# For the last pair of images, TensorE takes seven of the convolution's nine taps and VectorE two

## What is computed

```python
def block(x):
    # 1. depthwise 3x3 convolution whose nine taps depend on the image
    l = ln_over_channels(x)
    wt = softmax(max(l) @ w2.T + b2 - (mean(l) @ w1.T + b1), axis of length 1)   # 9 per image and channel
    x = x + (conv3x3(l, wt) + bias + l)
    # 2. mixture of 8 experts, 2 per token; a token is one pixel with its 128 channels
    t = tokens(x); n = ln_over_channels(t)
    top_w, top_i = top_k(n @ Wg + bg, 2); top_w = softmax(top_w)
    t = t + (sum(top_w[e] * (gelu(n @ W1[e] + b1[e]) @ W2[e] + b2[e]) for e in top_i))
    return images(t)
```

## Time and profile before

| | before |
|---|---|
| median of 3 runs | 1597.68 us (1597.11 to 1598.95) |
| span of the profiled execution | 1597.2 us |
| PE (TensorE) busy | 1476.3 us, 92% |
| DVE (VectorE) busy | 1379.2 us, 86% |
| ACT (ScalarE) busy | 1069.8 us, 67% |
| POOL (GpSimd) busy | 973.9 us, 61% |
| first stage, hand-over included | to about 610 us |
| experts' tiles and the last transposes | from about 610 us to the end |

### The profile page before, as it was taken

The page is one execution under the profiler, slowest core; times in us unless marked ns, Lnnn a source line. Parts: engine busy times, 40 slices in busy tenths (PEclk is TensorE's granted clock), DMA queues, the critical chain, the costliest instruction groups (busy, mean ns, idle before and its releaser), DMA issues.

```text
span 1597.2 us, 45596 instructions
## 1 busy us (share of the span) xinstructions
PE 1476.3 (92%) x12254; PEld 1135.9 (71%) x12255; DVE 1379.2 (86%) x2725; ACT 1069.8 (67%) x2410; POOL 973.9 (61%) x1062
## 2 busy tenths in 40 slices
PE   5899999999998777999999999999999999999776
PEld 2344545454545426999999999999999999999654
DVE  2568888888888856999999999999999999999654
ACT  4577777777777415777777777777777777777400
POOL 1004556456545674777777777777777777777500
PEclk7999999999999757999999999999999999999866
DMA  4202122212121183111111111111111111110199
GB/s 136 80 27 67 60 76 66 68 58 79 62 69 50 41 141 74 43 44 44 47 47 45 42 38 47 44 47 41 47 47 41 49 43 47 47 44 8 39 403 399
DMA packets 62200, 115.77 MB, mean 72 GB/s; under 512 B 15551, under 2 KB 39259, under 8 KB 62154
## 3 DMA queue, kind: packets, MB, share of 16 engines
q1 hardware_dynamic: 37354, 62.28, 12.8%
q0 software_dynamic: 18176, 34.27, 6.9%
q10 hardware_dynamic: 6624, 18.69, 3.3%
HBM read 60.22 MB, written 58.61 MB: 74 GB/s over the span
## 4 chain that ended last, share of the span: by engine, by line
POOL 33%; issue 27%; PE 23%; ACT 7%; DMA 5%; DVE 3%; POOLq 1%; SPq 1%; ACTq 0%; DVEq 0%
POOL token_out L501 17%; PE psV L816 11%; POOL yt L496 7%; POOL xn L489 7%; DMA ye<-token_out 4%; PE psV L767 4%; ACT spent L597 3%; PE psT L801 2%; PE psA L758 2%; PE psG L803 2%; POOL rows_by_pair L471 2%; ACT cv L585 1%; ACT sq L553 1%; PE psV L995 1%; DMA stage<-in_L_ffn_W_dram 1%
## 5 line engine op out<-in xcount | busy, mean ns | idle before, releaser
L1309 DVE TENSOR_TENSOR gl<-g,gh 128x512 f16<-128x512 f32 x624 | 527.2, 884 | 13.3 <-ACT gh L701 6.2
L501 POOL DMA_INDIRECT token_out<-yt,rt x312 | 399.5, 1280 | 186.1 <-POOL yt L496 133.5
L471 POOL DMA_INDIRECT rows_by_pair<-rows,idx x256 | 271.7, 1061 | 322.0 <-issue 198.7
L816 PE MATMUL psV<-lp,diag 128*128 128x512 f32 x576 | 275.1, 610 | 18.7 <-ACT cv L585 17.6
L701 ACT ACTIVATE gh<-g 128x512 f16<-128x512 f32 x468 | 276.3, 624 | 17.2
L694 ACT ACTIVATE g<-psT 128x512 f32<-128x512 f32 x312 | 183.1, 597 | 107.3 <-DVE gl L1309 83.4
L694 ACT ACTIVATE g<-psV 128x512 f32<-128x512 f32 x312 | 185.1, 597 | 91.7 <-PE psV L935 80.7
L956 PE MATMUL psR<-wall,gh 128*128 x1248 | 222.7, 273 | 0.6 <-DVE ya L1326 0.6
L956 PE MATMUL psG<-wall,gh 128*128 x1248 | 222.7, 273 | 0.0
L957 PE MATMUL psG<-wall,gl 128*128 x1248 | 214.3, 219 | 0.0
L957 PE MATMUL psR<-wall,gl 128*128 x1248 | 214.3, 219 | 0.0
(11 more groups left out here) (210 smaller groups left out, 2951.6 us busy)
## 6 DMA issues: line engine op xcount, KB each, us to landing
rt<-rows_by_pair SPq DMA_DIRECT2D x156, 133.0 KB
xb<-in_x_dram SPq DMA_DIRECT2D x32, 512.0 KB, 3.5
ye<-token_out SPq DMA_DIRECT2D x32, 512.0 KB, 7.8
out_dram<-oe ACTq DMA_DIRECT2D x32, 512.0 KB, 8.5
token_out<-yt,rt POOLq DMA_INDIRECT x312
rows_by_pair<-rows,idx POOLq DMA_INDIRECT x256, 2.5
stage<-in_L_ffn_W_dram SPq DMA_DIRECT2D x1, 2048.0 KB, 8.6
rows_by_pair<-pad_rows SPq DMA_DIRECT2D x15, 133.0 KB
```

Of the source, the lines that this page charges most:

```text
L471: gp.indirect_dma_start(rows_dram, bass.IndirectOffsetOnAxis(ap=idx[p][:, b:b + 1].bitcast(U32), axis=0), rows[p][:, b, :], None).then_inc ...
L501: gp.indirect_dma_start(y_dram, bass.IndirectOffsetOnAxis(ap=rt[r][:, b, ID:ID + 1].bitcast(U32), axis=0), yt[r][:, b, :], None, bounds_ch ...
L816: ins = te.matmul(psConv.rearrange("p (h w) -> p h w", w=WW), diag[k][:, m, :], lp[j][:, y:y + HH // 2, dx:dx + WW], start=(m == 0), stop= ...
L1309: v.tensor_tensor(gl[side][q][:, cols], g[side][:, cols], gh[side][q][:, cols], ALU.subtract).then_inc(lo_done, 1)
```

## The change

For the last pair alone, both images have seven taps on TensorE (4, 1, 3, 5, 7, 0, 2) and two on VectorE (6, 8). All other pairs stay as they are. For pair 15 TensorE therefore gets 14 products for each image in place of 10 and 8, ScalarE makes 14 diagonals in place of 9, and VectorE takes 2 and 2 taps in place of 4 and 5. The two diag tiles grow to seven matrices each. In TensorE's queue, products go where the loops over taps stand: those of the first half before the ranks, those of the second image's second half after them.

```diff
+    END_PE = PE_TAPS + (MORE, 0, 2)
+    END_DVE = [k for k in range(TAPS) if k not in END_PE]
...
-        diag = [sb(f"diag{k}", [P, len(taps_pe[k]), P], held=phase_a) for k in range(2)]
+        diag = [sb(f"diag{k}", [P, len(END_PE), P], held=phase_a) for k in range(2)]
...
+        def pe_taps(st_, stage, k):
+
+            return END_PE if st_.last(stage) else taps_pe[k]
+
+        def dve_taps(st_, stage, k):
+
+            return END_DVE if st_.last(stage) else taps_dve[k]
...
-                for m, tap in enumerate(taps_pe[k]):
+                for m, tap in enumerate(pe_taps(st_, 2, k)):
...
-                dy, dx = divmod(taps_pe[k][m], 3)
+                taps_ = pe_taps(st_, 2, k)
+                dy, dx = divmod(taps_[m], 3)
...
-                        for m in range(2, len(taps_pe[k])):
+                        for m in range(2, len(pe_taps(st_, 2, k))):
                             conv(st_, k, 0, m)
                     if k == 1 and st_.on(4):
                         ranks(st_)
                     if st_.on(2):
-                        for m in range(len(taps_pe[0]) if k == 0 else N_PE - 2):
+                        for m in range(len(pe_taps(st_, 2, k)) - 2 * k):
                             conv(st_, k, 1, m)
...
-                            conv(st_, 1, 1, N_PE - 2 + quarter)
+                            conv(st_, 1, 1, len(pe_taps(st_, 2, 1)) - 2 + quarter)
...
+                taps_ = dve_taps(st_, stage, k)
                 if first == 0:
-                    c_win.begin_at(st_.count(stage, len(taps_dve[0]) + len(taps_dve[1]) - 2, k * (len(taps_dve[0]) - 1)))
+                    c_win.begin_at(st_.count(stage, len(taps_dve[0]) + len(taps_dve[1]) - 2, k * (len(dve_taps(st_, stage, 0)) - 1)))
                     dve.wait_ge(x_used, n + 1)
-                for m in range(first, end):
-                    dy, dx = divmod(taps_dve[k][m], 3)
+                for m in range(first, min(end, len(taps_))):
+                    dy, dx = divmod(taps_[m], 3)
...
-                    if m < len(taps_dve[k]) - 1:
+                    if m < len(taps_) - 1:
                         c_win.link(ins)
                     else:
                         ins.then_inc(x1_ready, 1)
```

More of the change, by code:

```diff
@@ L813, in conv @@
                         pe.wait_ge(cv_ready, st_.count(2, 4, 2 * k + h))
-                dy, dx = divmod(taps_pe[k][m], 3)
+                taps_ = pe_taps(st_, 2, k)
+                dy, dx = divmod(taps_[m], 3)
                 y = dy + h * HH // 2
                 ins = te.matmul(psConv.rearrange("p (h w) -> p h w", w=WW), diag[k][:, m, :], lp[j][:, y:y + HH // 2, dx:dx + WW],
-                                start=(m == 0), stop=(m == len(taps_pe[k]) - 1))
-                if m == len(taps_pe[k]) - 1:
+                                start=(m == 0), stop=(m == len(taps_) - 1))
+                if m == len(taps_) - 1:
                     ins.then_inc(conv_ready, 1)
@@ L1097, in window @@
                 j, n = 2 * st_.slot(stage) + k, st_.count(stage, 2, k)
+                taps_ = dve_taps(st_, stage, k)
                 if first == 0:
-                    c_win.begin_at(st_.count(stage, len(taps_dve[0]) + len(taps_dve[1]) - 2, k * (len(taps_dve[0]) - 1)))
+                    c_win.begin_at(st_.count(stage, len(taps_dve[0]) + len(taps_dve[1]) - 2, k * (len(dve_taps(st_, stage, 0)) - 1)))
                     dve.wait_ge(x_used, n + 1)
-                for m in range(first, end):
-                    dy, dx = divmod(taps_dve[k][m], 3)
+                for m in range(first, min(end, len(taps_))):
+                    dy, dx = divmod(taps_[m], 3)
                     ins = v.scalar_tensor_tensor(out=img(x1[j]), in0=lp[j][:, dy:dy + HH, dx:dx + WW],
-                                                 scalar=taps[st_.slot(stage)][:, taps_dve[k][m], k:k + 1],
+                                                 scalar=taps[st_.slot(stage)][:, taps_[m], k:k + 1],
                                                  in1=img(x1[j]), op0=ALU.mult, op1=ALU.add)
-                    if m < len(taps_dve[k]) - 1:
+                    if m < len(taps_) - 1:
                         c_win.link(ins)
```

## The result

| | before | after |
|---|---|---|
| median, 6 runs each | 1597.53 us (1597.11 to 1598.95) | 1603.15 us (1601.5 to 1603.4) |
| ratio, 95% interval | | 1.0034 (1.0022 to 1.0045) |
| span of the profiled execution | 1597.2 us | 1599.7 us |
| PE / DVE / ACT / POOL busy, us | 1476.3 / 1379.2 / 1069.8 / 973.9 | 1478.4 / 1372.7 / 1072.5 / 973.4 |

The change costs 0.34%, 5.6 us. The profiled execution took 1601.5 us, the quickest of the six, 1.8 above its span. Executions of the kernel before lie 1.7 to 3.1 above theirs (75 of them were timed beside the experiments), so its first profile, with a span of 1597.2, belongs to a run of at least 1598.9, the slow end of before's six.

The account below looks back on a forecast made before the run. Bound: TensorE's queue ahead of pair 13's ranks, then VectorE's routing, 48 back-to-back POOL scatters and the experts' loads. Terms 0.61 + 6.16 - 0.5 = +6.3 us gave 1604.0 us, range 1601.5 to 1606.6.

Parts of the forecast that it names:

- The chain view: End of convolution stage: VectorE's chain, not POOL's queue, sets the last scatters; +4.4 us, 1602.1; chance 0.05.
- Seven products at 0.88: TensorE's queue ahead of pair 13's ranks: seven added convolutions at full-clock price, all on the path, +6.16 us.
- Rival D: TensorE's first half of pair 15's first image: clock rises later, +3.8 us more, 1607.8; chance 0.05.
- The diagonals, +0.61: ScalarE before TensorE's first convolution: seven diagonals ready 0.61 us later than five, all on the path.
- The scatters' own pace, -0.5: POOL's last 48 scatters: 0.5 of 1.85 us returns, for the slower first scatter and five fewer products beside scatters.
- the second image's add was put 8.3 later: VectorE behind pair 13's ranks: pair 15's second-image add moves from 540.99 to about 549.2.
- pairs 14 and 15 were put 4.4 later: VectorE's remaining routing: three fewer second-image products turn 8.3 us later into 4.3 to 4.4 later for both pairs.
- 4 had been forecast: Pair 14's cover: routed at about 564, POOL comes to it at about 568, so 4 us.
- Cover 5 us: Experts' start: weights' low parts end at 612.1, the first turn of rows waits for xn until 617.
- Rival A: VectorE's products shut out POOL's scatters: five fewer give 6.6 us back against 6.8, about 1597.9, no change; chance 0.05.

Follow-up runs that it names:

- second profile of before: Unchanged kernel before, run once more for another profile: 1597.85 us against 1597.09 beside it, ratio 1.0003; profile span 1595.2 us.
- TensorE's part alone: Changed kernel, but VectorE keeps its nine taps for the last pair, so some count twice: 1603.33 us against 1597.6 for the kernel before, ratio 1.0042.
- VectorE's part alone: Changed kernel, but TensorE keeps five and four taps for the last pair, leaving some out: 1597.6 us against 1597.6 for the kernel before, ratio 1.0000.
- POOL held up alone: Kernel before with ten small GpSimd operations on a spare tile ahead of pair 14's scatter: 1603.15 us against 1597.09, ratio 1.0042.
- the second set: Changed kernel run again unedited beside the kernel before: 1602.2 us against 1597.6, ratio 1.0030; median spans 1600.4 and 1595.4.
- first image alone: Change applied only to the last pair's first image: 1599.58 us against 1597.62 for the kernel before, ratio 1.0015.
- the kernel before with ranks and place first: Kernel before, pair 13's ranks ahead of the second image's turn, place, number, weigh ahead of the first image's add: 1597.64 us against 1597.09, ratio 1.0001.

## Why the prediction was right

**Path and sign.** TensorE's queue ahead of pair 13's ranks, then routing, then 48 scatters without a gap, then the loads: each link up to the last scatter moved by the same 5.3 to 5.5 us in the profile after, and xn by 5.3 against the second profile of before; the run with TensorE's part alone has the whole loss, VectorE's part alone has none of the gain, and POOL held up alone gives the loss again. The chain view's entry into POOL at 569.14 was rightly left aside: pair 15's routing moved 3.4 us ahead in the run with VectorE's part alone, and the scatters didn't follow.

**Size.** 6.3 was forecast, 5.6 and 4.6 were measured (5.0 in the spans of the second set). The terms:
- Seven products at 0.88, 6.16 in all, measured 1.05 + 1.72 + 2.58 = 5.35. Of the 0.8 less, 0.7 is the clock, which rose 3.0 us after the first convolution and not 4.2, and 0.1 the price (0.86). Rival D named the right quantity and the wrong direction. The Trainium skill (TensorE: Matmul & The Clock Gate, Part 1: The HAM clock gate) says the switching point moves from run to run; it did, and here it fell earlier. The first group lost 1.3 to 2.2 us to the lower clock in the seven profiles with ten records in it (5.81 to 6.75 instead of 4.56) and 1.2 to 1.9 in the six with fourteen (7.49 to 8.21 instead of 6.28). So the 0.7 is chance between two executions, not shown to be an effect of the change.
- The diagonals, +0.61: TensorE's first product started 2.21 us after ScalarE's first diagonal instead of 1.63, so 0.58.
- The turn between the second and the third group took 2.09 us instead of 2.41, which no term had and whose cause isn't shown; and the first product began only 0.35 later, since the step itself began 0.23 earlier in this execution. With these, 5.35 + 0.58 - 0.32 - 0.23 gives the 5.39 of the ranks.
- The scatters' own pace, -0.5, was wrong and measured +0.16. Two scatters are left at 1.02 beside products instead of five, which gives back 0.15; but the second image's add now makes one scatter 0.42 longer (548.48, 1.39), where it was 0.20 before (541.88, 1.17). The pause after pair 13's first scatter was put down half to VectorE; but with VectorE idle the pause grew from 1.57 to 1.86 just as the first scatter shrank from 1.26 to 0.96. From start to start it is 2.82 or 2.83 us in every profile of this study. It is POOL's own, and its cause isn't shown.
- Ranks later by 5.39, last scatter by 5.49 in the first pair of profiles.
- Behind the ranks, the second image's add was put 8.3 later and came 6.8 later, pairs 14 and 15 were put 4.4 later and came 3.4 and 3.0 later. None of it is on the path: POOL came to pair 14 4.1 us after its routing, and 4 had been forecast.

The forecast was 0.7 too high by the clock and 0.7 too low by the scatters' pace. That the two cancel is luck.

**The step that was wrong** is the cover at the experts' start, "the first turn of rows waits for xn ... Cover 5 us". It rested on one execution in which the last scatter landed 3 us late. In the second profile of before the weights are the bound, by about 0.6 us. So the first 0.6 us of any delay of the scatters is hidden (xn began 5.3 later in the changed kernel, the first turn 4.7), which takes the forecast nearer to what was measured, and the cover in the changed kernel was 1.7 us (610.85 + 0.7 against 613.28), not 5. Since the weights stayed just ahead there, the sign and nearly the size survived; in four of the experiments the weights were the bound, three times by themselves and once (first image alone) by holding up xn.

**Rival A** was priced too high, and rightly given little chance, but the reading against it, "the trace doesn't agree with it", was wrong. Products do shut scatters out. In the kernel before the first of the five products from 542.24 ends at 543.53, the scatter that started at 543.35 ends at 544.37, 0.84 later; the next product ends at 544.85, the next scatter at 545.68, and so on. Each scatter waits for a product's end. It costs 0.05 only because a product comes every 1.31 us and a scatter every 1.27 by itself: the cadence of 1.32, which was read as freedom, is VectorE's. The add shows it in the open, since nothing keeps step with it: in the kernel before with ranks and place first it ends at 542.33, and the scatter of 541.17 takes 1.99 and ends at 543.16, again 0.83 later. Beside the low parts of the weights a scatter takes up to 1.50. The Trainium skill (SBUF — State Buffer, SBUF: two separate sides) describes a port pair that VectorE and GpSimd lock against each other for a whole instruction; the trace agrees with it, for the products, the add and the low parts alike. What fails of rival A is the price: VectorE's part alone takes five products away and gives nothing.

## What to carry to other kernels

Before moving work from one engine to another at the end of a pipeline, follow the path to the queue that drains last, and ask which engine releases its first entry; work put ahead of that release is paid in full, and work taken from the other engine gives nothing. A chain view that enters a queue in its middle should be checked against that engine's timeline: if there is no idle time there, the queue's start is what counts. Take two profiles before calling a cover safe: the runner-up here was in truth ahead by 0.6 us, and one late DMA hid it. And to see whether one engine holds up another, compare when their instructions end, not only how long they take: two engines with nearly the same pace can run in lockstep with hardly a longer duration to show for it.

## What the runs showed of the hardware

TensorE's clock stayed at 0.50 through a long stretch of work. Busy times by stretch of the changed kernel:
```profile
574.00:603.00 29.00, 29.00 (x30) 6.99 (x28) 13.05 (x56) 4.07 (x7) 21.98 (x24) 0.50 1.01 190
```
These are the shift products, float32, of 512 columns, every second one with only 8 rows of weights. TensorE shows as busy all the time and was still granted 1.2 GHz for 29 us, while the convolutions, float32 too, were granted 2.4 GHz after 3.0 us. What of the products made the difference wasn't tried; at twice the clock the 32 us of them would be 16, an estimate from the two levels, and the weights would be no bound.

A scatter by GpSimd takes 0.97 us by itself. Of the 3328 in the thirteen profiles 633 took more than 1.1 us, and 632 of these ended 0.84 us after the end of a VectorE instruction, to 0.015 us. Such were the add and the products of the convolution, the low parts of the weights, and a few smaller ones; all of them read two inputs from SBUF. Of the scatters that started well inside an instruction of VectorE (0.1 us behind its start, 0.15 ahead of its end), all 237 in an add and 1071 of 1084 in a product ended so, and none of 109 in an instruction that reads PSUM: those took 0.96 to 0.97. GpSimd's xn is held up likewise, 1.07 and 1.80 us beside the low parts (second profile of before, TensorE's part alone) instead of 0.45.
